# Differential attention and a routed expert layer on one core: x arrives transposed, attention and join share a block, part of the routing moves

## The reference, cut to what matters

```python
# x: (2, 2048, 256), 4096 tokens; 16 heads of two 16-wide score pairs; 8 experts, 2 of them per token
Q, K, V = x @ Wq, x @ Wk, x @ Wv                       # Q and K are 512 wide, V is 256 wide
attn = softmax(Q1 @ K1.T / 4) - lamb * softmax(Q2 @ K2.T / 4)
o = layernorm((attn @ V) @ Wo) * gamma + beta
x1 = layernorm(x + o)                                   # the "join"
logits = (layernorm(x1) * rn_g + rn_b) @ router_w.T + router_b
top_w, top_idx = top_k(logits, 2); top_w = softmax(top_w)
for e in experts:                                       # dense in the reference
    h = layernorm(x1) * ln_g[e] + ln_b[e]
    y += combine[:, e] * (gelu(h @ w1[e] + b1[e]) @ w2[e] + b2[e])
out = layernorm(x1 + y)
```

## Time and profile before

| what | us |
|---|---|
| median of 3 runs | 3260.45 (3259.64 to 3260.81) |
| the profiled execution, its own time | 3255.12 |
| its span in the trace | 3253.4 |
| TensorE busy | 3089.5 (95%) |
| VectorE busy | 2738.8 (84%) |
| ScalarE busy | 2494.6 (77%) |
| GpSimd busy | 438.1 (13%) |

### The profile page before, as it was taken

How to read it: one execution, slowest core, us unless ns; L and a number is a source line. 1 busy time by engine, 2 the same in 40 slices (tenths; PEclk the granted TensorE clock), 3 DMA queues, 4 the chain that set the end, 5 groups by cost and what they waited for, 6 DMA issues and landing times. The chain is left out here.

```text
span 3253.4 us, 72428 instructions
## 1 busy us (share of the span) xinstructions
PE 3089.5 (95%) x29291; PEld 1389.6 (43%) x29292; DVE 2738.8 (84%) x2907; ACT 2494.6 (77%) x4641; POOL 438.1 (13%) x633
## 2 busy tenths in 40 slices
PE   8989999999999999999999999999999858999995
PEld 4423333333333333333333333333332647999995
DVE  3599999999999999999999999999996683433343
ACT  3369999999999999999999999999999432333333
POOL 3000000000000000000000000000000534555554
PEclk9989999999999999999999999999999978999998
DMA  5620101111010101111010101111000751222224
GB/s 167 160 50 8 28 22 29 24 27 28 9 31 21 28 9 29 39 25 28 21 31 8 28 22 28 22 30 28 8 12 21 271 200 30 36 36 37 37 37 123
DMA packets 100076, 148.72 MB, mean 46 GB/s; under 512 B 21480, under 2 KB 66400, under 8 KB 98112
## 3 DMA queue, kind: packets, MB, share of 16 engines
q1 hardware_dynamic: 83872, 125.84, 15.3%
q0 software_dynamic: 15904, 18.66, 3.6%
HBM read 84.16 MB, written 60.29 MB: 44 GB/s over the span
## 5 line engine op out<-in xcount | busy, mean ns | idle before, releaser
L743 DVE TENSOR_REDUCE half_max<-scores 128x2 f32<-128x1024 f32 x2016 | 2296.0, 1216 | 9.4 <-PE scores L616 4.1
L706 ACT ACTIVATE probs<-bank 128x512 f32<-128x512 f32 x4012 | 2141.8, 595 | 140.9 <-PE bank L629 43.2
L686 PE MATMUL bank<-probs,V 128*32 128x256 f32 x16384 | 1309.1, 391 | 44.5 <-ACT probs L706 42.6
L616 PE MATMUL scores<-K,Q 48*128 48x512 f16 x4032 | 789.2, 388 | 7.5 <-DVE half_max L743 5.2
L629 PE MATMUL bank<-Q,K 50*128 50x512 f16 x4012 | 789.7, 380 | 0.0
L686 PEld LDWEIGHTS bank<-probs,V 128*32 128x32 f32 x16384 | 322.5, 108 | 582.1 <-issue 516.8
L616 PEld LDWEIGHTS scores<-K,Q 48*128 48x128 f16 x4032 | 193.1, 92 | 841.5 <-DVE half_max L743 540.0
L629 PEld LDWEIGHTS bank<-Q,K 50*128 50x128 f16 x4012 | 371.2, 94 | 183.2 <-ACT probs L706 4.7
L585 POOL TENSOR_SCALAR max_parts<-row_max 128x16 f16<-128x16 f32 x64 | 16.2, 253 | 2082.7 <-DVE row_max L749 2082.7
L1596 ACT ACTIVATE h<-u 128x1024 f32<-128x1024 f32 x71 | 75.0, 1056 | 260.3 <-DVE u L1640 260.3
L1559 PE MATMUL pre<-xgT,w 128*128 128x128 f32 x2272 | 267.2, 276 | 2.8 <-ACT xgT L1590 2.8
(11 more groups left out here) (191 smaller groups left out, 1177.4 us busy)
## 6 DMA issues: line engine op xcount, KB each, us to landing
attended<-att SPq DMA_DIRECT2D x64, 256.0 KB, 2.8
W<-in_L_ffn_w_dram SPq DMA_DIRECT2D x16, 1024.0 KB, 6.7
heads<-attended SPq DMA_DIRECT2D x7, 2048.0 KB, 10.6
Q<-q_parts SPq DMA_DIRECT2D x96, 128.0 KB, 5.8
K<-k_parts SPq DMA_DIRECT2D x96, 128.0 KB, 6.3
q_parts<-parts SPq DMA_DIRECT2D x64, 128.0 KB, 2.4
k_parts<-parts SPq DMA_DIRECT2D x64, 128.0 KB, 3.0
xs<-in_L_attn_x_dram SPq DMA_DIRECT2D x8, 512.0 KB, 4.9
```

The costliest lines, as they stand in the source:

```text
L616: mm = nc.tensor.matmul(scores[:, b, h, :], Q[p][r, c, up, t * P:(t + 1) * P], K[p][r, up, kc * TC:(kc + 1) * TC], start=True, stop=True)
L686: mm = nc.tensor.matmul(banks[att_bank[s // KB]][32 * u:32 * u + 32, q], V[wp][:, wk, u // 2, :], probs[:, 4 * s % RING + u, q], start=(wk ...
L706: nc.scalar.activation(probs[:, i % RING, :], banks[tile_bank[i]][:], ACT.Exp, scale=SCALE).then_inc(exp_done, 1)
L743: nc.vector.tensor_reduce(half_max[lc % 2][:, :, up, t, kc], scores[:, b], AX.X, ALU.max).then_inc(max_done[b], 1)
```

## The change

It has three parts.

**x transposed.** The host passes x a second time as `x_cols`, transposed. SyncE loads a chunk of it straight into `xT` (COLS_AT is 2); `turn_x` and `copy_xT` are gone. The values get PSUM banks of their own.

```diff
+            def load_cols(n):
+                sp.dma_start(xT[n % 2][:], x_cols.rearrange("(k p) t -> p k t", p=P)[:, :, n * TC:(n + 1) * TC]
+                             ).then_inc(cols_loaded[n % 2], 16)
-            load_x(0)
+            load_cols(0)
             sp.dma_start(wv[:], Wv.rearrange("(k p) f -> p k f", p=P)).then_inc(wv_loaded, 16)
+            load_x(0)
             sp.dma_start(bet[:], row(beta, D)).then_inc(bet_loaded, 16)
+            load_cols(1)
-                            sp.wait_ge(x_turned, n + 2)
+                    if i == COLS_AT and 1 <= n < NC - 1:
+                        sp.wait_ge(v_ready, 2 * n)
+                        load_cols(n + 1)
             for n in range(NC):
-                pe.wait_ge(xT_ready, KD * (n + 1))
+                pe.wait_ge(cols_loaded[n % 2], 16 * (n // 2 + 1))
                 for i in range(ITEMS):
-                    if i == TURN_AT and n + 1 < NC:
-                        turn_x(n + 1)
```

```diff
+                    if it == PAIRS - 1 and lc == CH + 1:
+                        sp.wait_ge(v_copied, 2 * PAIRS)
+                        for p in range(2):
+                            sp.wait_ge(att_stored[p], 16 * HALFWAY * CH + 1)
+                        load_heads(0)
+                        load_heads(1)
+            sp.wait_ge(pv_done, STEPS + 1)
+            load_xb(0)
+            load_xb(1)
+            load_heads(2)
```

The setup of lambda and the router runs in the last pair: VectorE's part behind its last maxima, ScalarE's exponential and TensorE's three small products before step STEPS - 8:

```diff
+                        if it * RS + j == SETUP_AT:
+                            pe.wait_ge(exp_done, UNITS * PAIRED)
+                            pe.wait_ge(rw_mulled, 1)
+                            for f in range(KD):
+                                nc.tensor.transpose(turn_x[:, 0, f * E:(f + 1) * E], rw_scaled[:, f * P:(f + 1) * P], ident[0:E, 0:E])
+                            pe.wait_ge(rb_ready, 1)
+                            pe.wait_ge(consts_set, 3)
+                            nc.tensor.matmul(lgp[:, 0, :], rb_ones[:], rb_diag[:], start=True, stop=True).then_inc(rw_turned, 1)
```

```diff
+                if k == 0:
+                    numbers()
+                if k == DUOS + 3:
+                    top_two(DUOS - 1, slice(0, NT - 2))
+            top_two(DUOS, slice(NT - 2, NT))
...
+            pool.wait_ge(share_ready, 1)
+            nc.gpsimd.tensor_tensor(share[1][:], share[0][:], eg[:], ALU.mult).then_inc(pool_chain, 1)
...
+            nc.gpsimd.tensor_tensor(comb[:], part_of[0][:], part_of[1][:], ALU.add).then_inc(comb_ready, 1)
+            pool.wait_ge(ends_ready, 1)
+            for e in range(E):
+                nc.gpsimd.tensor_scalar(past[e][:], tau[:], last_end[:, e:e + 1], None, ALU.is_ge).then_inc(pool_chain, 1)
+            for d in (4, 2, 1):
...
+                for e in range(d):
+                    nc.gpsimd.tensor_tensor(past[e][:], past[e][:], past[e + d][:], ALU.add).then_inc(pool_chain, 1)
...
+            for r in range(2):
+                for t in range(NT):
+                    if t % HB == 0:
+                        act.wait_ge(tile_placed, (r * NT + t) // HB + 1)
+                    nc.scalar.activation(tile_hot[:, r, t, :], tile_hot[:, r, t, :], ACT.Copy, scale=token[:, t:t + 1]
+                                         ).then_inc(scaled_ready, 1)
...
-                    chain.wait()
-                    nc.vector.tensor_tensor(tile_hot[:, r, ts, :], tile_hot[:, r, ts, :],
-                                            token_h[:, ts].rearrange("p (t o) -> p t o", o=1).to_broadcast((P, HB, NTL)),
-                                            ALU.mult).then_inc(hot_ready, 1)
```

More of the change, by code:

```diff
@@ L159, in stage_project @@
         NL = 6 + len(lams)
+        cols_loaded = [sem(f"cols_loaded{i}") for i in range(2)]
         first_ready, first_done = sem("first_ready"), sem("first_done")
@@ L279, in _ @@
         def _(act):
[L280 to L286, removed]
             def copy_values(n):
@@ new lines, in stage_attend @@
+        ve1, rs1, nb1 = ([sb(f"{n}1_{i}", [P, 2, 2], F32) for i in range(2)] for n in ("ve", "rs", "nb"))
+        neg1 = [sb(f"neg1_{i}", [P, 2], F32) for i in range(2)]
+        token_major = scores[:].rearrange("p j h (u d) -> p j (h u) d", d=32)
+        turn_a, prod = (banks[att_bank[n]][:].rearrange("p (j d) -> p j d", j=2) for n in (RC - 2, RC - 1))
+        loose = [n for n in range(4) if n not in att_bank[RC - 2:]]
+        turn_x = banks[loose[0]][:].rearrange("p (j d) -> p j d", j=2)
@@ new lines, in stage_attend @@
+        lgp = banks[loose[1]][:, 0:2 * E].rearrange("p (j e) -> p j e", j=2)
+        SETUP_AT = STEPS - KB // 2
+        late = [K[1][:, u].bitcast(F32) for u in range(2)]
+        pick, rank = ([late[n][:, r * NT * E:(r + 1) * NT * E].rearrange("p (t e) -> p t e", e=E) for r in range(2)]
+                      for n in range(2))
+        lg2 = late[0][:, 2 * NT * E:3 * NT * E].rearrange("p (t e) -> p t e", e=E)
+        first = [late[1][:, (2 + r) * NT * E:(2 + r) * NT * E + NT] for r in range(2)]
@@ L607, in _ @@
+            for k in range(DUOS + 2):
+                if k < DUOS:
+                    add_pairs(k)
+                if 1 <= k < DUOS + 1:
+                    deviation(k - 1)
+                if k >= 2:
+                    deviations(k - 2)
         @block.tensor
@@ L733, in _, with normalise, copy_att, copy_xh @@
                         copy_att(it, j // KB)
+            def normalise(k, kind, dst, stored, ready):
+                i, q = k % 2, k // 2
+                if kind == 1:
+                    act.wait_ge(nb1_ready, k + 1)
+                    act.wait_ge(z_ready, 2 * (k + 1))
+                if k % 2 == 0 and q >= 2:
+                    act.wait_ge(stored[q % 2], 16 * (q // 2))
+                    if kind == 1:
+                        act.wait_ge(xh_turned, 2 * (q - 1))
+                for j in range(2):
+                    nc.scalar.activation(dst[q % 2][:, 2 * i + j, :], z[i][:, j, :], ACT.Identity,
+                                         scale=rs1[i][:, kind, j:j + 1], bias=nb1[i][:, kind, j:j + 1]).then_inc(ready, 1)
+            def copy_att(k):
+                act.wait_ge(att_turned, k + 1)
+                if k >= 2:
+                    act.wait_ge(y_ready, k - 1)
+                nc.scalar.copy(attT[k % 2][:], turn_a).then_inc(attT_ready, 1)
+            def copy_xh(k):
+                act.wait_ge(xh_turned, k + 1)
+                if k >= 2:
+                    act.wait_ge(logits_ready, k - 1)
+                nc.scalar.copy(xhT[k % 2][:], turn_x).then_inc(xhT_ready, 1)
+            for k in range(DUOS + 4):
+                if 1 <= k < DUOS + 1:
+                    copy_att(k - 1)
+                if k >= 4:
+                    copy_xh(k - 4)
+                if 3 <= k < DUOS + 3:
+                    normalise(k - 3, 1, xh, xh_stored, xh_ready)
+                    normalise(k - 3, 0, x1, x1_stored, x1_ready)
         @block.vector
@@ L1206, in stage_route @@
         base = sb("base", [P, E], F32)
-        past = sb("past", [P, NTL, E], F32)
         owner = sb("owner", [P, NTL], F32)
+        past = [sb(f"past{e}", [P, NTL], F32) for e in range(E)]
         took = [sb(f"took{i}", [P, NT, E], F32) for i in range(2)]
@@ L1336, in _ @@
             step(nc.vector.tensor_scalar(den[:], eg[:], 1.0, None, ALU.add))
-            step(nc.vector.reciprocal(share[0][:], den[:]))
-            step(nc.vector.tensor_tensor(share[1][:], share[0][:], eg[:], ALU.mult))
-            for r in range(2):
-                chain.add(nc.vector.tensor_tensor(part_of[r][:], hot[r][:], over_e(share[r][:]), ALU.mult))
-            chain.wait()
-            nc.vector.tensor_tensor(comb[:], part_of[0][:], part_of[1][:], ALU.add).then_inc(comb_ready, 1)
+            nc.vector.reciprocal(share[0][:], den[:]).then_inc(share_ready, 1)
             dve.wait_ge(counted_ready, 1)
```

690 lines of the change are left out of this document (312 added, 378 removed).

## The result

| | before | after |
|---|---|---|
| device time, median | 3260.6 us | 3243.2 us |
| range of its runs | 3259.6 to 3263.9 | 3242.2 to 3248.1 |
| the profiled execution (span) | 3255.1 (3253.4) | 3248.1 (3246.4) |

The ratio is 0.9952, 95% interval [0.9939, 0.9964]: 16 us faster, where 20.9 were forecast. A second set of runs of both kernels gave 0.9952 again, [0.9938, 0.9965]. The time lies inside the range. It is also that of rival B almost to the tenth, which is partly luck: B keeps the forecast's gain in counting, and that one did not come (experiment 4).

The account below looks back on a forecast made before the run. VectorE bounds attention and TensorE the experts, both untouched; the change shortens projection, seam, join's end and routing. Terms -4.0 - 7.4 - 3.8 - 1.4 - 1.7 - 2.6 = -20.9 give a median of 3239.5 us, 8-in-10 range 3229 to 3249.

Parts of the forecast that it names:

- x transposed: Projection: loading x as columns removes TensorE's transposes, part of the saving lost in stalls; -4.0 us, bounds -9 and 0.
- rival B: Projection: x columns compete with the stores, so the 4.0 go into longer waits in chunks 1 and 4; 3243.5 us, chance 0.2.
- The start: Projection's start: first transposes no longer stand before the weights' scale, and chunk 1's stall ends earlier; -1.5 us.
- The seam: Between attention and join: setup made earlier and heads already loaded, so TensorE goes on at once; -7.4 us.
- Top two: Join's end: top two of 240 elements during the last round, then 16, and no constants before "both"; -3.8 us.
- Counting: Routing: fp16 counting products and shares on GpSimd bring the totals' copy 1.4 us behind "both"; -1.4 us.
- Owners: Routing: owners move from VectorE to GpSimd, wanted only after the passes; -1.7 us, lower end 0.
- Tokens: Routing's eight passes: ScalarE multiplies in the tokens in 64 operations of 0.26 us, TensorE waiting for it; -2.6 us.
- Rival A: Routing's passes: ScalarE at 0.395 us per operation makes them 26 us, +6.2 instead of -2.6; 3248.3 us, chance 0.15.
- Rival C: Routing: the weights' load becomes the bound and cuts the passes' gain at -5; 3237 us, chance 0.1.
- D: Projection becomes bound by DMA, 4.2 MB more costing 21.6 us and TensorE stalling in every chunk; 3269.5 us, chance 0.03.
- E: Join starts early but waits 5 us in round 4 for its third heads load; 3244.5 us, chance 0.05.

Follow-up runs that it names:

- experiment 4: The changed kernel with TensorE doing the two counting products before the transposition of the loaded rows: 3242.73 us, ratio 0.9951 to the kernel before.
- experiment 10: The changed kernel with GpSimd's first addition of beta waiting until VectorE has scaled the weights: 3244.11 us, ratio 0.9952 to the kernel before.
- experiment 11: The changed kernel with the setup of lambda and router moved behind attention's last product, in the same block: 3245.99 us, ratio 0.9953 to the kernel before.
- experiment 6: The changed kernel with the owners on VectorE as in the kernel before, none on GpSimd: 3245.85 us, ratio 0.9957 to the kernel before.

## Why the prediction was near, step by step

- **x transposed, forecast -4.0: wrong in size; measured about -1.3.** The forecast has four parts up to attention's first scores. These are their means, of three profiles with rows and seven with columns:
  - *The start, -1.5: failed, -0.4.* I had the stall's end move "only with the start", and took 1.5 for that. It moved from 42.5 to 42.1. GpSimd's second shift comes behind its constants, and these wait for VectorE's scale of the weights, which came only 0.36 us earlier in the profiles shown (15.52 for 15.88). Where VectorE's step did not meet GpSimd's addition (experiment 10), the constants began at 14.6 to 15.2 and the stall ended at 41.5 to 41.9. TensorE's first projection, which I expected about 1 us earlier, came from 1.0 later to 2.2 earlier (15.1 to 18.3 against 17.3 in the mean).
  - *The transposes of chunks 2 to 4, 3.0 at TensorE: 2.4.* From the stall's end to the wait for the first group it needs 62.3 us instead of 64.7.
  - *That wait, longer by 1.0 and 1.5: right, 2.4.* 5.6 instead of 3.3, for SyncE's issues moved by 1.4 only and K took 1.0 longer from issue to scores.
  - *Chunks 5 and 6, -2.0: failed, -0.8.* I had priced no clock behind the wait. The products behind the first early scores took 3.7 us instead of 2.8 in the mean, at the lower level for most of it.

  Rival B, "the 4.0 go into longer waits in chunk 1 and 4", is nearer: these waits grew from 2.3 to 4.6 and from 3.3 to 5.6. But B says that nothing is left, and most of this growth was in my sum.
- **The seam, -7.4: right.** -7.7, and the setup between the last steps made the last attention chunk 28.53 instead of 28.37 us (0.2 for my 0.3; 28.36 in experiment 11, where it stands elsewhere). In three profiles that chunk took 29.9 to 30.0: the clock fell there as well, to a granted 0.50 from 2511 to 2513 in the profile shown.
- **Top two, -3.8: right within 0.4.** -3.4. The small operations took 0.21 each in step as forecast; the error is the block's end, 0.54 instead of 0.28, and the last logits, 5.06 instead of 4.93 behind those of round 14.
- **Counting, -1.4: wrong sign, +0.95.** The failing step is "What is left is both, gap, ScalarE's exponential, sum and reciprocal". These ended 1.39 us behind both, as priced. I never asked what stands ahead of the products in TensorE's order; experiment 4 shows it: the wait for the loaded rows, 2.4 us at the totals.
- **Owners, -1.7: right in kind, -1.4, net -1.0** with what GpSimd costs VectorE and ScalarE (experiment 6). This is the lower end I had named, in part.
- **Tokens, -2.6: right,** -2.85. ScalarE at 0.252 each was the bound and TensorE waited for it. The estimate from the Trainium skill (ScalarE: Activation LUTs, What ACT_TABLE_LOAD costs) had been 0.246; the trace agrees within 3%. Rival A, at the pair's 0.395, is out.
- **Rival C** did not occur: from the codes' copy to the end is the same in both kernels. **D** neither, nor **E**: the rounds take 98.7 at full clock, as before.

The sum of the measured terms is -1.3 - 7.7 + 0.2 - 3.4 + 0.95 - 1.4 - 2.85 = -15.5, and the ratio says -15.6. That they agree so well is luck: the ratio's interval is 12 to 20 us, and attention as a whole, 2351.5 us in both profiles of before, has 2351.1 to 2355.4 and a median of 2352.4 in the twelve others, 0.7 more than the setup explains. Two terms, off by 2.4 and 2.7 in the same direction, are nearly all of the 5.4 between the sums. The median came out 3.7 above the forecast; the other 1.7 lie within what medians of this kernel scatter (3258.6 to 3260.7 for the kernel before). One sum in the prediction is off: the upper bounds of its terms add up to -2, not -5.

## What to carry to other kernels

Whenever a step gets its input earlier, read what stands ahead of it in the order of every engine that it uses, and what has covered that; here a load that 7.5 us of other work had hidden became the bound. Time saved ahead of a wait counts only up to that wait: find what ends it and whether it moves too. And take a second profile of both kernels before you compare stretches of 1 or 2 us, since one pair of profiles here told less than half of the gain.

## What the runs showed of the hardware that I had not expected

- A VectorE operation on two numbers took 2.26 us instead of 0.16 when a GpSimd addition over 128x1024 had begun 0.1 us before it, and ended with it. The conversion of tau in the join took 1.29 us for its neighbours' 0.15 to 0.22, beside GpSimd's work. In the passes 576 and 1024 elements took 0.88 and 1.35 us beside GpSimd and 0.74 and 1.21 without. One addition of beta in the way was worth up to 3 us at the first projection, and 0.4 to 1.0 at the end of chunk 1's stall.
- The same join rounds took 98.7, 100.2, 101.6 or 102.9 us in different executions, by how long the granted clock was at the lower level around TensorE's idle time of about 2.3 us between the transposes of rounds 0 and 1. What decides this in an execution stays open; no kernel here tried to remove that idle time.
